# Attention probabilities transposed in VectorE blocks and through DRAM, with the turn put in another order

## The reference, cut to what matters

```python
# layer 0: 8 heads of 32, b = graph
nx = ln(x, ln1_g, ln1_b)
q, k, v = heads(nx @ wq + bq), heads(nx @ wk + bk), heads(nx @ wv + bv)
bias = where(adj > 0, 0.1 * edge * adj, -inf)
attn = softmax(q @ k.T / sqrt(32) + bias)
x1 = x + (merge(attn @ v) @ wo + bo)
x2 = x1 + gelu(ln(x1, ln2_g, ln2_b) @ w1 + b1) @ w2 + b2
# layer 1: one head
w = softmax(where(adj == 0, -inf, (x2 @ Wq) @ (x2 @ Wk).T / 16))
out = layer_norm(x2 + w @ (x2 @ Wv) @ Wo + bo1, gamma, beta)
```

## Time and profile before

| | us |
|---|---|
| median of 3 runs (lowest, highest) | 915.56 (914.96, 917.57) |
| span of the profiled execution | 913.2 |
| TensorE busy | 892.7 (98%) |
| VectorE busy | 693.0 (76%) |
| ScalarE busy | 638.4 (70%) |
| GpSimd busy | 389.6 (43%) |

### The profile page before, as it was taken

The page is one execution under the profiler, slowest core; times in us unless marked ns, Lnnn a source line. Parts: engine busy times, 40 slices in busy tenths (PEclk is TensorE's granted clock), DMA queues, the critical chain, the costliest instruction groups (busy, mean ns, idle before and its releaser), DMA issues.

```text
span 913.2 us, 22669 instructions
## 1 busy us (share of the span) xinstructions
PE 892.7 (98%) x7623; PEld 808.4 (89%) x7623; DVE 693.0 (76%) x2580; ACT 638.4 (70%) x1888; POOL 389.6 (43%) x258
## 2 busy tenths in 40 slices
PE   8989999999999999999999999999999999999996
PEld 7878898989989898998989989898998989898795
DVE  7786868779696877959778695877969687786736
ACT  5784958768495876949577694866859587684842
POOL 4633243635516354352645425363551536444222
PEclk9999999999999999999999999999999999999998
DMA  8101000100101010000100101010010100000001
GB/s 266 36 1 36 1 24 25 37 24 23 34 0 34 23 34 23 14 24 19 34 23 23 34 0 34 23 34 23 23 34 0 34 23 29 11 24 2 1 24 35
DMA packets 29743, 26.29 MB, mean 29 GB/s; under 512 B 1142, under 2 KB 29452, under 8 KB 29708
## 3 DMA queue, kind: packets, MB, share of 16 engines
q1 hardware_dynamic: 29692, 25.83, 9.1%
q10 hardware_dynamic: 16, 0.00, 0.0%
HBM read 17.44 MB, written 8.39 MB: 28 GB/s over the span
## 4 chain that ended last, share of the span: by engine, by line
PE 87%; DVE 4%; ACT 4%; issue 3%; POOL 1%; POOLq 0%; DVEq 0%; ACTq 0%
PE bank L364 22%; PE bank L366 21%; PE bank L365 21%; PE bank L521 5%; PE bank L513 3%; PE bank L532 3%; PE bank L634 3%; PE bank L659 3%; ACT bank L934 2%; PE bank L615 2%; PE bank L554 1%; PE bank L458 1%; PE bank L652 1%; DVE p_s L1296 1%; ACT bank L965 1%
## 5 line engine op out<-in xcount | busy, mean ns | idle before, releaser
L934 ACT ACTIVATE bank<-p_s,neg_max 128x128 f32<-128x128 f32 x512 | 181.7, 355 | 11.1 <-DVE neg_max L1296 11.0
L1707 POOL TENSOR_TENSOR rstd<-ve,minus_half 128x4 f32<-128x4 f32 (+1 forms) x49 | 54.2, 1106 | 300.5 <-DVE ve L1259 300.5
L364 PE MATMUL bank<-w_hi,hT_hi 128*128 128x256 f32 x512 | 147.4, 288 | 0.0
L366 PE MATMUL bank<-w_hi,hT_lo 128*128 128x256 f32 x512 | 144.1, 281 | 0.0
L365 PE MATMUL bank<-w_lo,hT_hi 128*128 128x256 f32 x512 | 144.1, 281 | 0.0
L1296 DVE CUSTOM_DVE_ANT_0 p_s<-bank,bias 128x128 f32<-128x128 f32 x512 | 112.9, 288 | 3.2 <-PE bank L513 3.2
L1190 DVE TENSOR_TENSOR hT_lo<-bank,hT_hi 128x512 fp32r<-128x512 f32 (+1 forms) x151 | 95.7, 657 | 19.2 <-ACT hT_hi L877 19.0
L364 PE MATMUL bank<-n2T_hi,w_hi 128*128 128x512 f32 (+1 forms) x272 | 108.3, 398 | 0.5 <-DVE hT_lo L1190 0.5
L366 PE MATMUL bank<-n2T_hi,w_lo 128*128 128x512 f32 (+1 forms) x272 | 103.8, 382 | 0.0
L365 PE MATMUL bank<-n2T_lo,w_hi 128*128 128x512 f32 (+1 forms) x272 | 103.7, 381 | 0.0
L364 PEld LDWEIGHTS bank<-w_hi,hT_hi 128*128 128x128 f32 x512 | 96.4, 188 | 2.7 <-DVE hT_lo L1190 1.2
(11 more groups left out here) (228 smaller groups left out, 2441.4 us busy)
## 6 DMA issues: line engine op xcount, KB each, us to landing
xs<-in_x SPq DMA_DIRECT2D x15, 512.0 KB, 3.8
out<-y SPq DMA_DIRECT2D x14, 512.0 KB, 3.0
adj_i<-in_adj SPq DMA_DIRECT2D x15, 256.0 KB, 2.8
out<-y SPq DMA_DIRECT2D x3, 256.0 KB, 2.2
x2T_f<-in_L_gnn_w SPq DMA_DIRECT2D x1, 512.0 KB, 6.6
tT<-in_L_gnn_w SPq DMA_DIRECT2D x1, 512.0 KB, 8.2
y<-in_L_gnn_w SPq DMA_DIRECT2D x1, 512.0 KB, 6.4
vo<-in_L_gnn_w SPq DMA_DIRECT2D x1, 512.0 KB, 8.3
```

What stands on the lines that cost most here:

```text
L364: mm(out, a_hi, b_hi, start=first, stop=False)
L366: return mm(out, a_lo, b_hi, start=False, stop=last)
L934: last = run(bank[r][:, NODES * place:NODES * place + NODES], p_s[:, r, place, :], ACT.Exp, scale=-1.0, bias=neg_max[:, r, place:place + 1 ...
L1707: P.tensor_tensor(t["rstd"][:, 0:k], t["ve"][:, 0:k], minus_half[:, 0:k], ALU.pow).then_inc(ln_pool[n], 1)
```

## The change

For groups 2 to 16 TensorE's transposes and the four copies of each pair are gone. VectorE transposes each 32 x 32 block of p_s into the tile pT (`blocks`, one instruction of 128 x 512 for each r). SyncE stores pT to a DRAM tensor `parked` in four DMAs of 256 KB, one for each 32 partitions, and loads it back in one DMA of 1 MB, which puts the blocks in place. Pair 0 is loaded to pT and pair 1 to p_s. As both pairs use pT as the tile that is stored, the loads wait for both stores, and pair 1's first block transpose waits for the landing of pair 0's store. Groups 0 and 1 stay as they were.

The turn is in another order on every engine. Both pairs' scores and softmax are now made in the turn in which the group is gp; the attends come one turn later. k and q stand ahead of the down product, both attends stand behind pair 0's scores and the first half of the down product, and pair 1's scores behind the second half. The first `biased` of pair 0 waits for `pe_av`, both attends of ga, since p_s holds the probabilities of ga's pair 1 until then (that wait was in the kernel before too, where the attends were long over). `scores(g, 1)` waits for pair 0's last `divided`, as both use banks 0 to 3. Banks are dealt anew.

```diff
-                pe.wait_ge(act_pT, 2 * (pair0(g) + q) + 2)
-                pe.wait_ge(dve_pT, 2 * (pair0(g) + q) + 2)
+                if by_blocks(g):
+                    pe.wait_ge(park_load[q], 16 * g - 16)
...
+            def blocks(g, q, r):
+                dve.wait_ge(dve_p, 4 * (pair0(g) + q) + r + 1)
+                if r == 0:
+                    if q == 0:
+                        dve.wait_ge(pe_av, pair0(g) - 1)
+                    else:
+                        dve.wait_ge(park_store[0], 64 * g - 64)
+                V.transpose(pT[:, r, :, :].rearrange("p b (l i) -> p l b i", l=4),
+                            p_s[:, r, :, :].rearrange("p l (b j) -> p l b j", j=32)).then_inc(dve_blocks, 1)
...
+            def store_blocks(g, q):
+                sp.wait_ge(dve_blocks, blocks_done(g, q, HPT - 1))
+                for a in range(NODES // 32):
+                    sp.dma_start(parked[q].rearrange("r b j a x -> j (r b) a x")[:, :, a, :],
+                                 pT[32 * a:32 * a + 32, :, :, :].rearrange("p r b x -> p (r b) x")).then_inc(park_store[q], 16)
+
+            def load_blocks(g, q):
+                for u in pairs(g):
+                    sp.wait_ge(park_store[u], 64 * g - 64)
+                sp.dma_start(pT_of[q][:, :, :, :].rearrange("p r a x -> p r (a x)"),
+                             parked[q].rearrange("r b j a x -> (b j) r (a x)")).then_inc(park_load[q], 16)
...
+            # SyncE
+            def turn(gp, ga, gc):
+                store_blocks(ga, 1)
+                load_blocks(ga, 0)
+                load_blocks(ga, 1)
+                if not is_last(gp):
+                    load_adj(gp + 1)
+                store(gc)
+                store_blocks(gp, 0)
+                if not is_last(gp):
+                    load_x(gp + 1)
...
+            # TensorE, turn(gp, ga, gb)
+                for j in range(6):
+                    mlp_up(gb, j, True)
+                norm_transpose(gp)
+                mlp_up(gb, 6, True)
+                mlp_up(gb, 7, True)
+                project_k(gp, 0)
+                project_k(gp, 1)
+                project_q(gp, 0)
+                project_q(gp, 1)
                 mlp_down(gb, 0)
+                scores(gp, 0)
+                attend(ga, 0)
+                attend(ga, 1)
+                mlp_down(gb, 1)
+                if size(gp) > 2:
+                    scores(gp, 1)
+                x2_transpose(gb)
+                out_project(ga, 0)
+                out_project(ga, 1)
+                t_project(gb)
+                project_v(gp, 0)
+                scores1(gb, True)
+                vo_project(gb, 0, True)
+                vo_project(gb, 1, True)
+                n2_transpose(ga, True)
+                p1_transpose(gb)
```

More of the change, by code:

```diff
@@ L154, in build, with by_blocks, pT_part, blocks_done @@
         pT_of = (pT, p_s)
-        avT_of = ([a[:, :, :] for a in avT], [h[:, 0, :].rearrange("p (h n) -> p h n", h=4) for h in hT])
+        parked = nc.dram_tensor("parked", (2, HPT, NODES // 32, 32, NODES // 32, NODES), f32).ap()
+        def by_blocks(g):
+            return not (isinstance(g, int) and g < 2)
+        def pT_part(g, q, r, place):
+            t = pT_of[q]
+            return t[:, r, :, 32 * place:32 * place + 32] if by_blocks(g) else t[:, r, place, :]
+        def blocks_done(g, q, r):
+            return 4 * (pair0(g) - pair0(2) + q) + r + 1
+        avT_of = ([a[:, :, :] for a in avT], [h[:, 0, :].rearrange("p (h n) -> p h n", h=4) for h in n2T])
         def home(n, g):
@@ L334, in _ @@
                 load_row(dst, src, row_load)
[L335 to L346, removed]
+            load_adj(2)
+            load_x(2)
+            store_blocks(2, 0)
+            load_adj(3)
+            load_x(3)
+            def turn(gp, ga, gc):
[8 more added lines that the diff above has]
+                    load_x(gp + 1)
+            turn(3, 2, 0)
+            with sp.Fori(3, GROUPS - 3) as g:
+                turn(g + 1, g, g - 2)
+            turn(GROUPS - 2, GROUPS - 3, GROUPS - 5)
+            turn(GROUPS - 1, GROUPS - 2, GROUPS - 4)
+            load_blocks(GROUPS - 1, 0)
+            store(GROUPS - 3)
             for q in range(2):
@@ L455, in norm_transpose @@
                 pe.wait_ge(ln_dve[1], ln_end(g))
+                if not (isinstance(g, int) and g < 3):
+                    pe.wait_ge(dve_p, 4 * pair0(g))
                 for t in range(KT):
@@ L491, in project_v @@
                     pe.wait_ge(*((act_l1, 2), (dve_h, 3))[q])
+                elif isinstance(g, int) and g == 2 and q == 1:
+                    pe.wait_ge(act_p1T, 1)
+                elif not (isinstance(g, int) and g < 3):
+                    pe.wait_ge(*((dve_x1, pair0(g) - 1), (dve_vo, g - 2))[q])
                 for b in (2 * q, 2 * q + 1):
                     for t in range(KT):
-                        last = mm3(bank[v_at(g, q)][:, row(b)], both(nxT, ALL, t, nodes(b)), both(wv_p, ALL, t),
+                        last = mm3(bank[at("v", g)[q]][:, row(b)], both(nxT, ALL, t, nodes(b)), both(wv_p, ALL, t),
                                    t == 0, t == KT - 1)
@@ L576, in mlp_up @@
                     pe.wait_ge(dve_y, graph0(g))
+                    if isinstance(g, int) and g == 1:
+                        pe.wait_ge(act_v, pair0(g + 2))
                 elif j >= 4:
@@ L593, in mlp_down @@
                                    i == 0, i == HT - 1)
-                last.then_inc(pe_down, 1)
+                if graphs[-1] == 1:
+                    last.then_inc(pe_down, 1)
             def last_down(g, b, tiles):
@@ L1069, in first_turn @@
+                t_copy(gb)
+                if whole:
+                    exps(gp, 1, 2)
+                v_copy(gp, 0)
+                if whole:
+                    exps(gp, 1, 3)
+                exps1(gb)
+                vo_copy(gb)
+                n2T_copy(ga)
+                p1T_copy(gb)
+                if whole:
+                    v_copy(gp, 1)
             def first_turn():
@@ new lines, in turn @@
+                nxT_low(gp)
+                for j in range(5, HT):
+                    h_low(gb, j)
+                for r in range(HPT):
+                    biased(gp, 0, r)
+                attn_low(ga, 0)
+                divided(gp, 0, 0)
+                blocks(gp, 0, 0)
+                divided(gp, 0, 1)
+                blocks(gp, 0, 1)
+                residual2(gb, 0)
+                divided(gp, 0, 2)
+                divided(gp, 0, 3)
+                attn_low(ga, 1)
+                blocks(gp, 0, 2)
@@ new lines, in turn @@
+                residual2(gb, 1)
+                blocks(gp, 0, 3)
+                if whole:
+                    biased(gp, 1, 0)
+                    biased(gp, 1, 1)
+                x2T_low(gb)
+                residual1(ga, 0, True)
+                if whole:
+                    biased(gp, 1, 2)
+                residual1(ga, 1, True)
+                if whole:
+                    biased(gp, 1, 3)
+                sums2(ga, 0)
+                sums2(ga, 1)
+                moments(2, ga)
```

483 lines of the change are left out of this document (169 added, 314 removed).

## The result

| | before | after |
|---|---|---|
| median (lowest, highest), us | 915.5 (915.0, 917.6) | 1012.0 (1010.7, 1013.2) |
| span of the profiled execution | 913.2 | 1008.8 |
| one loop turn | 54.15 | 60.22 |
| TensorE idle in it | none | 6.05 |

After divided by before is 1.105, 95% interval 1.103 to 1.107: 10.5% slower, and 10 us above the forecast of 1002.

A forecast was written before the change was run, and what follows sets the result against it. A closed VectorE-TensorE ring was to bound the turn: 11.35 + 14.7 + 33.2 = 59.25 us, 59.7 with the clock. Start, turns and ends (110.2 + 26.1 + 716.4 + 33.7 + 49.9 + 63.7) gave span 1000, median 1002; range 962 to 1035.

The forecast's parts named there:

- stretch 1: VectorE from the last residual to the split norm (statistics, moments, norms, low parts): 11.35 us of a turn.
- stretch 2: TensorE from k to the attends' end (k, q, half the down product, scores, attends), with handovers: 14.7 us.
- stretch 3: VectorE from pair 0's first biased to the last residual, with eight block transposes: 33.2 us, 33.7 with the clock.
- the clock: TensorE's clock falls to half rate for some 3 us after its idle time, adding 0.5 us a turn.
- The ring: Closed path of waits between VectorE and TensorE: a turn is three stretches in a row, 59.25 us, 59.7 with the clock.
- VectorE's wait: VectorE idle before pair 0's first biased until the attends end: about 12.6 us a turn.
- the hole: TensorE idle before pair 1's scores, waiting for VectorE's fourth division of pair 0: 4.1 us a turn.
- Rival 1: TensorE stays the bound: turn 50.8 us, time 867; 5%, with everything between 867 and 912.
- The ends of the range: Bounds on one VectorE block transpose's price: 0.60 us with no drain, 1.14 if strided access is half again as slow.
- Rival 3: The clock doesn't fall in TensorE's idle time before pair 1's scores: 14 x 0.5 us less, 995; 14%.
- Rival 2: DRAM is late: store and loads take over 25.5 us together; at 30, 59 us more, 1060; 9%.
- that handover: Pair 0's store must land within 8.6 us, before pair 1's first transpose; 6 us was forecast, narrowly enough.

The follow-up runs named there:

- e1: The changed kernel with both attends and pair 0's scores moved ahead of the first half of the down product on TensorE; 934.7 us.
- e5a: The changed kernel with eight further unused statistics instructions on VectorE behind attn_low of pair 0, in stretch 3; 1048.1 us.
- e5b: The changed kernel with eight further unused statistics instructions on VectorE just ahead of pair 0's first biased, where it waits for the attends; 1009.8 us.
- e10: e8 with norm 2 ahead of pair 1's first block transpose and the copy of vo ahead of its second, on VectorE; 896.2 us.
- e9: The changed kernel with each VectorE block transpose cut from 128 x 512 to 128 x 32, probabilities left mostly untransposed; 974.4 us.
- e6b: The changed kernel with 14 unused identity matmuls on TensorE ahead of pair 1's scores, to fill its idle time there; 999.5 us.
- e4: The changed kernel with the changes of e1 and e3 together, and GpSimd's last reciprocal deviation behind its bias; 915.0 us.
- e7: e4 with VectorE's copy of t ahead of norm 2's second statistics and the MLP's second low part ahead of norm 1; 907.5 us.
- e8: e7 with VectorE's layer-1 biased ahead of pair 1's first block transpose and of norm 2; 901.2 us.
- e3: The changed kernel with the last layer norm's statistics, moments and norm on VectorE moved from ahead of the split norm into its wait for the attends; 993.1 us.

## Why the prediction was right

**The sum by its steps.** All in us:

| step | predicted | measured |
|---|---|---|
| VectorE's last block transpose before the turns ends | 110.2 | 112.2 |
| first `biased` behind stretches 1 and 2 | 136.3 | 137.69 |
| stretch 1 | 11.35 | 11.88 |
| stretch 2 | 14.7 | 14.92 |
| stretch 3, with the clock | 33.7 | 33.42 |
| loop turn | 59.7 | 60.22 (mean of twelve 60.17) |
| from the thirteenth `biased` to the end | 147.3 | 149.1 |
| span | 1000 | 1008.8 |

Of the 8.8 of difference, twelve turns carry 5.6, the start 1.4 and the end 1.8. The median lies 3.2 above its span, where I had put 2.4.

**The ring.** The mechanism held. e1, e5a and e5b tell it from an engine that is full: VectorE's wait of 13.0 (predicted 12.6), the hole of 3.68 (4.1), and work that costs nearly everything in stretch 3 and nothing in stretch 2. Rival 1, TensorE stays the bound, is refuted in the changed kernel (54.17 busy of 60.22) and comes true in e10, where the ring is out of the way. Even then its turn is 51.58 and not the 50.8 that I had from the earlier trace rows: taking out 3.34 us of transposes took 2.9 off TensorE's list (54.15 to 51.23).

**The block transpose.** I took 0.84 on the ring, between 0.60 and 1.14, with a start that is 0.24 late. It starts 0.13 late (504.76 to 505.49 for a sum that costs 0.60). One division with its transpose is 1.53 (504.60 to 506.13), the one ahead of it 1.57; less the 0.81 of a division alone that is 0.72 to 0.76. The record is 0.71. The two transposes of the turn that stand apart from their divisions keep the queue 0.62 and 0.77 (508.91 to 509.53, 510.11 to 510.88). The ends of the range could have been closer: the row of any 128 x 512 operation was the right neighbour. By the difference of e9, 0.50 us for 480 columns, a column costs 1.04 ns and the rest of the instruction 0.18. The estimate from the Trainium skill (VectorE: DVE Perf Modes, The three transpose paths), four bf16 squares of 311 ns, 1.24 us, isn't borne out for this f32 instruction. The prediction said that the trace before bore out neither figure of that page; it could say so of TensorE's 390 ns alone, since that trace had no block transpose.

Nor is the page's order of the two paths, VectorE's 311 ns ahead of TensorE's 390, that of the queues here. The 16 transposes of a pair kept TensorE 1.67 us, and VectorE's two copies behind them 1.2 (0.60 each): 2.9 on both engines. The four block transposes keep VectorE alone 2.9 (4 x 0.72). What the change buys is the 1.67 on the engine that was full.

**What cancelled.** Eight transposes at 0.76 make stretch 3 0.6 us shorter than forecast. The clock makes it about 0.5 longer than forecast: VectorE waits 0.96 for x2T_hi, since scores and x2's transposes took 2.09 and 1.97 in place of 1.17 and 1.09. I had the fall last some 3 us, after the earlier trace rows, and cost 0.5; the rows show five to six us at or near half rate, and e6b shows about 1.0. The term of the sum that was too small is this one. That stretch 3 came out within 0.3 of the forecast is luck in so far as these two errors have opposite signs. A third reading was off without a cost: ScalarE lost 1.2 us a turn (38.88 to 37.71) and not 2.4, but no term of the sum rests on it. Rival 3, the clock doesn't fall, was priced at 995; e6b measured 999.5 with the clock held up.

**Stretch 1** was 0.53 too short in the sum, for a reason not named there: the last norm is 1.82 long beside GpSimd's conversion of the adjacency (480.41 to 483.3) and 1.38 in e4, e7, e8 and e10, where GpSimd is idle meanwhile; the conversion of 2.07 in these rows is 1.93 there too. That it is GpSimd's work that slows it is read from these traces alone; no run has only that changed.

**DRAM.** Rival 2 was refuted. Store and loads take 14.4 of the 26.05 us from the first store to the first attend (470.82 to 496.87; predicted 16 of 25.5): the four stores are issued within 2.8 us and land in 4.1 each, the loads in 5.5 and 7.7. No attend waits for them. VectorE's one wait for a store, 1.38, is in the part before the turns, where pair 1's transposes follow pair 0's at once; the prediction had called that handover narrow.

**Where my reading of the ring was too simple** only the experiments showed. Taking 3.8 us out of stretch 1 gave 1.5 to 1.7 (e3), taking 4.0 out of stretch 3 gave 2.5 to 2.7 (e9), and in e1 the clock came back but a wait for the down product took its place. Each stretch is the longest of several chains, and the second longest was one to two us behind. Adding was nearly exact (e5a: 2.4 to 2.5 for 2.6), removing is not. The forecast had to find the longest chain of one given order and not what would follow if it were shortened, and so this didn't touch it; the expected times of e1, e3, e4, e7 and e9 it did.

## What to carry to other kernels

When two engines each have a long list and a turn is longer than either's work, look for the closed path: where A's first product waits for B's last, and B's for something in the middle of A's list. The remedy is the order and not the amount of work, and here moving 5.8 us of products in each turn was worth 77 us. Then don't expect a stretch that you shorten to give back all of it: here 5.6 us gave 5.5 (e1), 3.8 gave 1.5 to 1.7 (e3) and 4.0 gave 2.5 to 2.7 (e9). Close the holes of the fullest engine from the trace one by one, until it has none.

## What the runs showed of the hardware

- A hole of 3.68 us on TensorE, all else busy, brought its granted clock to 0.50 for some five to six us behind it, and one of 2.87 us in e9 to 0.55 and 0.59 in the next four us. Holes of up to 1.2 us (e1), or of 0.55, 0.62 and 1.10 in one turn (e6b), left it at 1.00.
- A block transpose of 128 x 512 f32 on VectorE, with strided output, is 0.71 us long, where a plain copy or sum is 0.69. It keeps the queue 0.62 to 0.77 us (0.72 to 0.76 just behind the division that it reads), and a plain operation 0.60. One of 128 x 32 is 0.21 long.
- 128 x 128 f32 products against the identity, written as matmuls, cost TensorE 0.23 us each (two instructions of 0.11); as transposes in a row 0.10.
- In the median, a 256 KB store from 32 partitions, one of four issued within 2.8 us, lands in 4.1 us, and two overlapping loads of 1 MB in 5.5 and 7.7; the core's rate reached 408 GB/s in the loads (542 to 543 us of the changed kernel).
